# Pre-norm attention layer on one core: the weighting of the values five units behind the scores instead of three

## The chip, the core and the metric

The kernel runs on one core of one Trainium2 chip, as one program with one launch. The metric is the device time of that launch in microseconds (us). PE is the tensor engine, PEld its weight loads, ACT the scalar engine, DVE the vector engine, POOL the GpSimd engine, SP the engine that issues the DMAs (its queue is SPq in the rows).

## The reference

A pre-norm transformer layer over 4 sequences of 2048 tokens with 256 channels and 16 heads of 16 channels, all in float32. The mask is unusual: a query sees every key except the 17 from its own place back to 16 before it.

```python
def attn(x):
    qkv = einsum('bse,fe->bsf', x, in_proj_weight) + in_proj_bias
    q, k, v = split(qkv, 3)                 # 16 heads of 16
    scores = einsum('bhqd,bhkd->bhqk', q / sqrt(16), k)
    blocked = (j <= i) & (j >= i - 16)
    attn = softmax(where(blocked, -inf, scores))
    return einsum('bhqk,bhkd->bhqd', attn, v) @ out_proj_weight.T + out_proj_bias
x = x + attn(layernorm(x))
x = x + tanh(((layernorm(x) @ weight) @ aux_weight1) @ aux_weight2 + bias)
```

## The kernel before, in words

`first_batch` normalises and projects the first sequence; it ends 88 us into the span. `stream` does everything else. A guard at the end (`if_bad`) can call a slower exact path; it is not taken with these inputs.

**Units.** `stream` cuts the work into 16 steps (`NCH`), each 512 queries of one sequence. A step has 64 units (`STEP`): two passes of 8 heads (`hg`), each over 32 blocks of 64 keys (`KBLOCKS`). Unit `u` makes the scores of 512 queries against 64 keys for 8 heads. The text calls the place of a unit in its step `r` (0 to 63) and in its pass `i` (0 to 31).

- PE computes the scores of a unit in two halves, `score(u, 0)` and `score(u, 1)` (line 1183, 8 matmuls each), into two halves of one PSUM tile. It may overwrite a half once ACT has read that half of the unit before.
- ACT takes the exponential of each half (line 1160) into `probs`, a ring of 8 units (`RING`). It waits for the scores, and for the weighting of the unit that last held the ring slot.
- DVE zeroes the 17 blocked keys in the few units that hold them (`mask`, line 871; `i` of 15 to 23), two units behind.
- PE multiplies the exponentials by the values, `weigh(u)` (line 1202, 16 matmuls), and sums a pass of 32 units in the PSUM tile `outs`. The value rows have a column of ones, so `outs` also holds the sums of the softmax.
- After the last unit of a pass DVE copies `outs` to `raw` (`evacuate`, lines 879 and 880), and only then may the first `weigh` of the next pass write.

**The order is written out by hand.** Every engine walks through the same units in its own loop (`run_step`), and other work hangs at fixed values of `r`. On PE, a unit is `score(u, 0)`, then what `weighed_at(u)` names, then `score(u, 1)`, then a piece of a projection, if one is due. `weighed_at` sets how far the weighting lags: three units, with one unit without weighting after the end of a pass (`i` = 3, while DVE empties `outs`), four units behind until `i` = 12, and a double one at `i` = 13 that catches up.

**After a pass** (in step `step`, for step `f = step - 1` that has just ended): DVE empties the second pass at `r` = 3; SP moves `raw` out (`move_context`, 8 DMAs to `ctx_in` and 2 to `row_sums`), reads the sums back in another layout (line 722), and DVE inverts them at `r` = 8 (`invert`, lines 884 to 891). SP writes the inverses, reads them back spread over the channels, and DVE scales the context at `r` = 19 and 20. PE then projects it out from `r` = 23. SP issues in program order: after this chain it stores a result and loads the next inputs.

**Beside it, in steps 0 to 11**, the projection of the next sequence: PE turns the normalised input at `r` = 7 to 10 (`turn`, line 1230), DVE copies it to `s_xt` at `r` = 11 (`copy_turned`, line 924), and PE projects q and k from `r` = 12 (`project_qk`, line 1241), where its first matmul waits for that copy. DVE takes the four results at `r` = 17, 22, 37 and 42 (`take_qk`, line 935 onwards), and PE starts the next one in the same PSUM banks at `r` = 18, 33 and 38. `squash` on ACT (line 1152) is the tanh of an earlier step; DVE adds the residual at `r` = 10 (`add_squashed`, line 1048).

After unit 1023 PE has three units left to weigh; then the chain above runs once more with nothing beside it, followed by the output projection and the feed-forward part of the last step.

Of the kernel before, what the change touches and what calls it, by code (L numbers as in the profile page):

```python
# [1 line left out]

# [7 lines left out]
ALU = mybir.AluOpType  # L10
# [3 lines left out]
P = 128  # L14
# [37 lines left out]
NORM_AT = 49  # L52
F_TURN_AT = {True: (56, 57, 58, 59), False: (41, 42, 43, 44)}
# [476 lines left out]
def stream(nc, keep, lay, x, w1_t, a1_t, a2, q_parts, k_parts, row_sums, row_inverse, out):  # L530


    with ExitStack() as ctx:  # L533
# [51 lines left out]

        scored = sem("scored")
# [7 lines left out]
        floored = sem("floored")  # L594
# [8 lines left out]
        eps_added = sem("s_eps_added")  # L603
# [11 lines left out]
        v_added = sem("s_v_added")  # L615
        norms_ready = sem("s_norms_ready")
        norms_copied = sem("s_norms_copied")
        norms_added = sem("s_norms_added")
        max_done = sem("s_max_done")
        product_done = sem("s_product_done")  # L620
        worst_done = sem("s_worst_done")
        bound_done = sem("s_bound_done")
# [11 lines left out]
        y_added = sem("s_y_added")  # L634
# [3 lines left out]
        f_eps_added = sem("s_f_eps_added")  # L638
# [5 lines left out]
        f_added = sem("s_f_added")  # L644
        qk_added = sem("s_qk_added")
# [157 lines left out]
        def _(pool):  # L803
            bias = keep["bias_o"][:].unsqueeze(1).to_broadcast([P, TPC, EMB])

            def rsqrt(step):
                pool.wait_ge(stats_done, step + 1)
                pool.tensor_tensor(var_eps[:], mean_var[:, :, 1], keep["eps"][:], ALU.add).then_inc(eps_added, 1)
                pool.wait_ge(eps_added, step + 1)
# [12 lines left out]
            def f_rsqrt(c):  # L822
                pool.wait_ge(f_stats_done, c + 1)
                pool.tensor_tensor(f_var_eps[:], f_mean_var[:, :, 1], keep["eps"][:], ALU.add).then_inc(f_eps_added, 1)  # L824
                pool.wait_ge(f_eps_added, c + 1)
                pool.tensor_tensor(f_rstd[:], f_var_eps[:], keep["minus_half"][:], ALU.pow).then_inc(f_rstd_done, 1)  # L826

            def guard_of(b):

                pool.wait_ge(max_done, 2 * b + 2)  # L830
                pool.tensor_tensor(product[:], qk_max[:, 0:1], qk_max[:, 1:2], ALU.mult).then_inc(product_done, 1)
                pool.wait_ge(product_done, b + 1)
                pool.tensor_copy(keep["worst"][:, 0:2, b + 1], qk_max[:]).then_inc(worst_done, 1)
                pool.tensor_copy(keep["worst"][:, 2:3, b + 1], product[:]).then_inc(worst_done, 1)
                pool.tensor_tensor(bound[:], product[:], keep["half_power"][:], ALU.pow).then_inc(bound_done, 1)
                pool.wait_ge(bound_done, b + 1)
# [27 lines left out]
        def _(dve):  # L864
# [17 lines left out]
            def invert(c):  # L882
                dve.wait_ge(sums_in, c * 16 + 16)
                dve.tensor_scalar(sums_floor[:], sums[:], SUM_FLOOR, None, ALU.max).then_inc(floored, 1)
# [3 lines left out]
                dve.wait_ge(floored, c + 1)  # L888
# [39 lines left out]
            def take_qk(step, j):  # L928
                n = step * 4 + j
                dve.wait_ge(qk_ready, n + 1)  # L930
                if n >= 2:
# [4 lines left out]
                                  ).then_inc(qk_added, 1)  # L936
                dve.wait_ge(qk_added, n + 1)
# [12 lines left out]
            def take_v(step, half):  # L950
                b, qc = divmod(step + CPB, CPB)
                dve.wait_ge(v_ready, step * 2 + half + 1)
                if step >= CPB:
# [7 lines left out]
                        [P, 4, HALVES * HG, HD]), ALU.add).then_inc(v_added, 1)  # L961
                dve.wait_ge(v_added, step * 2 + half + 1)
# [3 lines left out]
            def take_norms(step):  # L966
# [5 lines left out]
                dve.tensor_copy(both, spare[0][0:HALF_P]).then_inc(norms_added, 1)  # L972
                dve.wait_ge(norms_added, 2 * step + 1)
                dve.tensor_tensor(both, both, spare[1][0:HALF_P], ALU.add).then_inc(norms_added, 1)
                dve.wait_ge(norms_added, 2 * step + 2)
# [17 lines left out]
            def add_attention(c, pair):  # L993
# [4 lines left out]
                                  ).then_inc(y_added, 1)  # L998
                dve.wait_ge(y_added, c * 2 + pair + 1)
# [35 lines left out]
            def add_f_bias(c, pair):  # L1035
                dve.wait_ge(f_ready, c * 2 + pair + 1)
                if c:
# [3 lines left out]
                                  keep["bias_f"][:].unsqueeze(1).to_broadcast([P, 2, EMB]), ALU.add).then_inc(f_added, 1)  # L1041
                dve.wait_ge(f_added, c * 2 + pair + 1)
# [7 lines left out]
            def run_step(step):  # L1050
# [3 lines left out]
                for r in range(STEP):  # L1054
# [45 lines left out]
                    if finishes:  # L1100
                        if r == 8:
# [67 lines left out]
        def _(pe):  # L1169
# [212 lines left out]
            for u in range(NCH * STEP, NCH * STEP + 3):  # L1382
# [677 lines left out]
```

## Time and profile before

| what | value |
|---|---|
| median of 3 runs | 2064.96 us (2062.73 to 2069.01) |
| the profiled execution's own time | 2062.95 us |
| its span, first to last instruction | 2058.0 us |
| first exponential starts / last one starts | 88.97 / 1992.8 us |
| ACT busy | 1924.7 us (94%) |
| PE busy | 1827.9 us (89%) |
| DVE busy | 696.1 us (34%) |
| POOL busy | 151.5 us (7%) |
| mean granted clock of TensorE | 0.981 of full speed |

Times in rows are from the span's start. Two instructions of ACT overlap at their ends, so that "mean ns of one" is more than busy time by count; the distance from start to start is what one costs. A number in brackets behind a row is the idle time of the engine before it, with what ended it. "x16" counts instructions merged into the row.

### The profile page before, as it was taken

Reading aid. Unit: us, or ns where it says so; the run is one execution under the profiler, and the core shown is the slowest. Engines: PE = TensorE matmul, PEld = TensorE weight load, DVE = VectorE, ACT = ScalarE, POOL = GpSimd, SP = SyncE. Lnnn points to the kernel's source line nnn. Section 1 sums busy time; section 2 is a strip of 40 time slices with the busy share of each in tenths; the row PEclk is TensorE's granted clock in tenths of the full one; section 3 lists DMA queues with packets and bytes.
Section 4 is the critical chain, followed back from the end, with each engine's and each line's share of the span. In section 5 each row is a group of like instructions: output and inputs, shape, how many; then the busy total and the mean of one; then the engine's idle time right before and its main releaser. Section 6 shows DMA issues by size and latency. Waiting matters only on the chain. (4 is left out here: it accounts for less than half of the span.)

```text
span 2058.0 us, 100762 instructions
## 1 busy us (share of the span) xinstructions
PE 1827.9 (89%) x47072; PEld 751.1 (36%) x47072; DVE 696.1 (34%) x1366; ACT 1924.7 (94%) x2106; POOL 151.5 (7%) x172
## 2 busy tenths in 40 slices
PE   6599899999999999999999999999998888898872
PEld 3233334343434334343443434343332323232321
DVE  5323332433344343434433343343322112121222
ACT  3499999999999999999999999999999999999970
POOL 1000000101010000101100010000000000000000
PEclk9799999999999999999999999999999999999995
DMA  3400102101230210202231110201111010101010
GB/s 118 137 27 23 58 26 59 36 18 55 58 100 27 58 37 18 64 25 61 57 82 45 30 61 17 60 27 54 54 54 48 13 42 12 47 16 47 8 29 24
DMA packets 93664, 94.39 MB, mean 46 GB/s; under 512 B 17514, under 2 KB 84522, under 8 KB 93234
## 3 DMA queue, kind: packets, MB, share of 16 engines
q1 hardware_dynamic: 93236, 87.84, 14.8%
q8 instruction: 372, 6.09, 1.3%
q14 instruction: 56, 0.46, 0.1%
HBM read 53.09 MB, written 26.25 MB: 39 GB/s over the span
## 5 line engine op out<-in xcount | busy, mean ns | idle before, releaser
L1160 ACT ACTIVATE probs<-scores 128x1024 f32<-128x1024 f32 x2048 | 1886.9, 1113 | 28.6 <-PE scores L1183 26.6
L1202 PE MATMUL outs<-probs,vs 64*32 64x512 f32 x16384 | 1076.5, 590 | 0.2 <-issue 0.2
L1183 PE MATMUL scores<-qs,ks 49*32 49x512 f16 x16384 | 838.6, 383 | 164.1 <-ACT probs L1160 142.9
L1183 PEld LDWEIGHTS scores<-qs,ks 49*32 49x32 f16 x16384 | 233.2, 89 | 1085.4 <-ACT probs L1160 1046.1
L1202 PEld LDWEIGHTS outs<-probs,vs 64*32 64x32 f32 x16384 | 301.2, 106 | 36.7 <-issue 11.3
L871 DVE TENSOR_TENSOR probs<-probs,allowed 128x320 f32<-128x320 f32 (+2 forms) x280 | 149.4, 537 | 308.2 <-ACT probs L1160 307.9
L1241 PE MATMUL spare<-s_xt,w_qkv 64*32 64x256 f32 x3072 | 121.4, 376 | 0.0
L1241 PE MATMUL spare<-w_o,ctx_in 64*32 64x256 f32 x2048 | 80.4, 384 | 21.0 <-DVE ctx_in L896 19.4
L820 POOL TENSOR_TENSOR s_squares<-s_qk_f 128x512 bf16<-128x512 f32 x48 | 61.3, 1278 | 353.0 <-DVE s_qk_f L938 353.0
L814 POOL TENSOR_TENSOR s_x<-s_x,bias_o 128x1024 f32<-128x1024 f32 x16 | 38.1, 2384 | 626.2 <-DMA s_x<-in_x 626.2
L1241 PE MATMUL spare<-w_ffn,s_f_xt 64*32 64x256 f32 x2048 | 81.6, 389 | 3.0 <-DVE s_pre L1043 1.6
L935 DVE TENSOR_SCALAR s_qk_f<-spare,bias_qk 128x512 f32<-128x512 f32 x48 | 36.1, 751 | 136.5 <-PE spare L1241 136.5
L997 DVE TENSOR_TENSOR s_x<-s_x,spare 128x512 f32<-128x512 f32 x32 | 22.0, 688 | 176.8 <-PE spare L1241 176.8
L1241 PEld LDWEIGHTS spare<-s_xt,w_qkv 64*32 64x32 f32 x3072 | 56.6, 106 | 26.9 <-issue 3.6
L1031 DVE COPY s_f_xt<-spare 128x512 f32<-128x512 f32 x32 | 20.6, 686 | 134.6 <-PE spare L1230 134.6
L1040 DVE TENSOR_TENSOR s_pre<-spare,bias_f 128x512 f32<-128x512 f32 x32 | 22.1, 691 | 130.0 <-PE spare L1241 130.0
L1152 ACT ACTIVATE s_pre<-s_pre 128x1024 f32<-128x1024 f32 x16 | 18.3, 1146 | 47.2 <-DVE s_pre L1043 47.2
L879 DVE COPY raw<-outs 128x512 f32<-128x512 f32 x32 | 22.1, 691 | 118.4 <-PE outs L1202 118.4
L1285 PE MATMUL spare<-w_qkv,s_xt 64*32 64x128 f32 x3072 | 61.4, 269 | 0.0
L1285 PEld LDWEIGHTS spare<-w_qkv,s_xt 64*32 64x32 f32 x3072 | 49.9, 106 | 15.5 <-issue 3.7
L1241 PEld LDWEIGHTS spare<-w_o,ctx_in 64*32 64x32 f32 x2048 | 37.4, 108 | 39.9 <-DVE ctx_in L896 20.3
L958 DVE TENSOR_TENSOR vs<-spare,bias_v 128x512 f32<-128x512 f32 x24 | 16.6, 692 | 102.5 <-PE spare L1285 102.5
(103 smaller groups left out, 770.5 us busy)
## 6 DMA issues: line engine op xcount, KB each, us to landing
qs<-q_parts SPq DMA_DIRECT2D x192, 64.0 KB
ks<-k_parts SPq DMA_DIRECT2D x192, 64.0 KB
ctx_in<-raw SPq DMA_DIRECT2D x256, 32.0 KB, 2.0
inverse<-row_inverse SPq DMA_DIRECT2D x32, 256.0 KB
s_x<-in_x SPq DMA_DIRECT2D x16, 512.0 KB, 7.2
out<-s_pre SPq DMA_DIRECT2D x16, 512.0 KB, 6.1
s_xin<-in_x SPq DMA_DIRECT2D x12, 512.0 KB, 7.8
q_parts<-s_parts SPq DMA_DIRECT2D x24, 256.0 KB, 2.3
```

Source lines behind the costliest of these rows:

```text
L814: pool.tensor_tensor(x2[:], x2[:], bias, ALU.add).then_inc(biased, 1)
L820: pool.tensor_tensor(squares[:, j], qk_f[:, j % 2], qk_f[:, j % 2], ALU.mult).then_inc(squared, 1)
L871: dve.tensor_tensor(tiles, tiles, keep_row, ALU.mult).then_inc(masked, 1)
L879: dve.tensor_copy(raw[:, 0], outs[:, 0])
L935: dve.tensor_scalar(qk_f[:, j % 2], spare[0][:], scale, bias_qk[:, j:j + 1], ALU.mult, ALU.add).then_inc(qk_added, 1)
L997: dve.tensor_tensor(tiles, tiles, spare[0][:].rearrange("p (t e) -> p t e", t=2), ALU.add).then_inc(y_added, 1)
L1040: dve.tensor_tensor(tiles, spare[0][:].rearrange("p (t e) -> p t e", t=2), keep["bias_f"][:].unsqueeze(1).to_broadcast([P, 2, EMB]), ALU.a ...
L1160: act.activation(probs[:, u % RING, 2 * slot:2 * slot + 2].rearrange("p c q -> p (c q)"), scores[:, 2 * slot:2 * slot + 2].rearrange("p c ...
L1183: last = pe.matmul(scores[cols, 2 * slot + e], ks[rows, group, keys], qs[rows, group], start=True, stop=True)
L1202: last = pe.matmul(outs[32 * c:32 * c + 32, side], vs[keys, at:at + 2 * HD], probs[keys, u % RING, c], start=(i == 0), stop=(i == KBLOCKS ...
L1241: last = pe.matmul(spare[part][32 * c:32 * c + 32, at:at + EMB], weights(rows, c), moving[rows], start=(k == 0), stop=(k == HALVES - 1))
L1285: last = pe.matmul(spare[part][32 * c:32 * c + 32, i * P:(i + 1) * P], xt[rows, k, keys], w_qkv[rows, k, 2 * EMB + side * P:2 * EMB + (sid ...
```

## The change

A new constant `LAG = 5` takes the place of the 3 in `weighed_at`, in the number of units left after the last scores, and in DVE's two places of `evacuate` (`r` 3 and 35 become 5 and 37) and of `invert` (`r` 8 becomes 10). The unit without weighting moves from `i` = 3 to `i` = 5, and the stretch that runs one unit further behind is now six behind, `i` = 6 to 12. The double one stays at `i` = 13. The diff also replaces a dozen semaphores, each of which an engine used to wait for its own last instruction, by one counter for DVE and one for POOL; each such wait still waits for the same instruction.

```diff
+LAG = 5
...
+        dve_step = sem("dve_step")
+        dve_steps = count(1)
+        pool_step = sem("pool_step")
+        pool_steps = count(1)
...
             i = position % KBLOCKS
             base = position - i
-            if i < 3:
-                found = [base - 3 + i]
-            elif i == 3:
+            if i < LAG:
+                found = [base - LAG + i]
+            elif i == LAG:
                 found = []
             elif i < 13:
-                found = [position - 4]
+                found = [position - LAG - 1]
             elif i == 13:
-                found = [position - 4, position - 3]
+                found = [position - LAG - 1, position - LAG]
             else:
-                found = [position - 3]
+                found = [position - LAG]
...
             def invert(c):
                 dve.wait_ge(sums_in, c * 16 + 16)
-                dve.tensor_scalar(sums_floor[:], sums[:], SUM_FLOOR, None, ALU.max).then_inc(floored, 1)
+                dve.tensor_scalar(sums_floor[:], sums[:], SUM_FLOOR, None, ALU.max).then_inc(dve_step, 1)
...
-                dve.wait_ge(floored, c + 1)
+                dve.wait_ge(dve_step, next(dve_steps))
...
-                    if finishes and r == 3:
+                    if finishes and r == LAG:
                         evacuate(f, 1)
-                    if r == 35:
+                    if r == KBLOCKS + LAG:
                         evacuate(step, 0)
...
-                        if r == 8:
+                        if r == LAG + 5:
                             invert(f)
...
-            for u in range(NCH * STEP, NCH * STEP + 3):
+            for u in range(NCH * STEP, NCH * STEP + LAG):
                 for w in weighed_at(u):
                     weigh(w)
```

How the instructions move. Lines of the changed kernel are 4 lower than those of the one before in this part of the file.

DVE at the start of step 2, from the end of the feed-forward bias to the copy of the turned input. Before:

```order
163 L908 BN_AGGR s_mean_var<-s_stats 128x2 x4
164 L879 COPY raw<-outs 128x512
165 L880 COPY raw<-outs 128x512
166 L915 TENSOR_SCALAR s_xin<-s_xin,s_mean_var,s_rstd 128x256 x4
167 L1040 TENSOR_TENSOR s_pre<-spare,bias_f 128x512
168 L1043 TENSOR_TENSOR s_pre<-s_pre,spare 128x512
169 L884 TENSOR_SCALAR sums_floor<-sums 128x64
170 L886 SCALAR_TENSOR_TENSOR sums_fine<-sums,sums_fine 128x64
171 L891 RECIPROCAL sums_inv<-sums_floor 128x64
172 L1048 TENSOR_TENSOR s_pre<-s_pre,s_x 128x1024
173 L924 COPY s_xt<-spare 128x8x64 x2
```

And with the change:

```order
164 L904 BN_AGGR s_mean_var<-s_stats 128x2 x4
165 L911 TENSOR_SCALAR s_xin<-s_xin,s_mean_var,s_rstd 128x256 x2
166 L875 COPY raw<-outs 128x512
167 L876 COPY raw<-outs 128x512
168 L911 TENSOR_SCALAR s_xin<-s_xin,s_mean_var,s_rstd 128x256 x2
169 L1036 TENSOR_TENSOR s_pre<-spare,bias_f 128x512
170 L1039 TENSOR_TENSOR s_pre<-s_pre,spare 128x512
171 L1044 TENSOR_TENSOR s_pre<-s_pre,s_x 128x1024
172 L880 TENSOR_SCALAR sums_floor<-sums 128x64
173 L882 SCALAR_TENSOR_TENSOR sums_fine<-sums,sums_fine 128x64
174 L887 RECIPROCAL sums_inv<-sums_floor 128x64
175 L920 COPY s_xt<-spare 128x8x64 x2
```

The copy of `outs` now stands between the two halves of the normalisation, and the inversion of the sums has passed the residual add: it is now the last thing ahead of the copy of the turned input.

PE at the end of `stream`, from the last units of scores to the output projection. Before:

```order
3363 L1183 MATMUL scores<-qs,ks 32x512 x16
3364 L1202 MATMUL outs<-probs,vs 32x512 x8
3365 L1183 MATMUL scores<-qs,ks 32x512 x8
3366 L1202 MATMUL outs<-probs,vs 32x512 x24
3367 L1241 MATMUL spare<-w_o,ctx_in 32x256 x64
```

And with the change:

```order
3359 L1179 MATMUL scores<-qs,ks 32x512 x16
3360 L1198 MATMUL outs<-probs,vs 32x512 x8
3361 L1179 MATMUL scores<-qs,ks 32x512 x8
3362 L1198 MATMUL outs<-probs,vs 32x512 x40
3363 L1237 MATMUL spare<-w_o,ctx_in 32x256 x64
```

A matmul of float32 stands in these lists once and in the trace twice, so one weighting is x8 here and x16 there. Five weightings instead of three now follow the last scores.

## Rows read from the trace of the kernel before

**Rows 1.** The page, busy time by engine.

```profile
PE 1827.9 (89%) x47072; PEld 751.1 (36%) x47072; DVE 696.1 (34%) x1366; ACT 1924.7 (94%) x2106; POOL 151.5 (7%) x172
```

**Rows 2.** Who waited for whom: total us, times, longest.

```profile
ACT probs L1160 <- PE scores L1183: 26.6, 8, 21.5
...
PEld outs L1202 <- ACT probs L1160: 0.4, 1, 0.4
```

**Rows 3.** Timeline of ACT: start, length, what, count [idle before].

```profile
88.97 8.36 ACT L1160 ACTIVATE probs<-scores 128x1024 f32<-128x1024 f32 x9 [21.47 <-PE scores L1183]
98.38 1.94 ACT L1160 ACTIVATE probs<-scores 128x1024 f32<-128x1024 f32 x2 [1.05 <-PE scores L1183]
100.65 34.23 ACT L1160 ACTIVATE probs<-scores 128x1024 f32<-128x1024 f32 x37 [0.33 <-PE scores L1183]
136.00 9.43 ACT L1160 ACTIVATE probs<-scores 128x1024 f32<-128x1024 f32 x10 [1.13 <-PE scores L1183]
...
583.10 1.15 ACT L1152 ACTIVATE s_pre<-s_pre 128x1024 f32<-128x1024 f32 x1
584.05 117.96 ACT L1160 ACTIVATE probs<-scores 128x1024 f32<-128x1024 f32 x128
```

**Rows 4.** Timeline of PE at the start of the stream.

```profile
95.94 1.93 PE L1202 MATMUL outs<-probs,vs 64*32 64x512 f32 x16
...
98.50 1.84 PE L1202 MATMUL outs<-probs,vs 64*32 64x512 f32 x16
```

**Rows 5.** Stretches there: busy of PE, PEld, DVE, ACT, POOL; granted clock; DMA share, GB/s.

```profile
94.00:96.00 2.00, 1.42 (x32) 0.38 (x32) 0.72 (x6) 2.00 (x3) 1.08 (x2) 0.50 0.02 7
...
100.00:102.00 2.00, 1.92 (x48) 0.43 (x32) 0.00 (x0) 1.67 (x3) 0.00 (x0) 0.97 0.00 0
```

**Rows 6.** Timeline at the end of the stream, PE, PEld and DVE.

```profile
1992.52 2.77 PE L1202 MATMUL outs<-probs,vs 64*32 64x512 f32 x48
1992.95 0.14 PEld L1202 LDWEIGHTS outs<-probs,vs 64*32 64x32 f32 x8 [0.29 <-issue]
1993.38 0.14 PEld L1202 LDWEIGHTS outs<-probs,vs 64*32 64x32 f32 x8 [0.29 <-issue]
...
1995.41 0.69 DVE L879 COPY raw<-outs 128x512 f32<-128x512 f32 x1 [9.41 <-PE outs L1202]
...
2013.29 1.29 DVE L896 TENSOR_TENSOR ctx_in<-ctx_in,inverse 128x512 f32<-128x512 f32 x2 [6.80 <-DMA inverse<-row_inverse]
```

**Rows 7.** Timeline of step 6, r = 2 to 12: DVE, SP and PE.

```profile
808.46 0.69 DVE L879 COPY raw<-outs 128x512 f32<-128x512 f32 x1 [1.23 <-PE outs L1202]
...
820.73 0.20 DVE L884 TENSOR_SCALAR sums_floor<-sums 128x64 f32<-128x64 f32 x1 [4.70 <-DMA sums<-row_sums]
...
820.98 0.55 DVE L891 RECIPROCAL sums_inv<-sums_floor 128x64 f32<-128x64 f32 x1
...
824.54 1.29 DVE L924 COPY s_xt<-spare 128x512 f32<-128x512 f32 x2 [1.58 <-PE spare L1230]
...
817.54 0.53 PE L1230 MATMUL spare<-ident,s_xin 64*32 64x64 f32 x32
...
827.42 0.40 PE L1183 MATMUL scores<-qs,ks 49*32 49x512 f16 x8
827.64 0.62 PE L1241 MATMUL spare<-s_xt,w_qkv 64*32 64x256 f32 x16
```

**Rows 8.** The same two places in step 9, the one with the earliest sums.

```profile
1175.21 0.20 DVE L884 TENSOR_SCALAR sums_floor<-sums 128x64 f32<-128x64 f32 x1 [2.80 <-DMA sums<-row_sums]
...
1184.01 0.62 PE L1241 MATMUL spare<-s_xt,w_qkv 64*32 64x256 f32 x16
```

**Rows 9.** Timeline of step 6, r = 36 to 39, PE and DVE.

```profile
870.77 1.04 PE L1202 MATMUL outs<-probs,vs 64*32 64x512 f32 x16
...
872.60 0.75 DVE L935 TENSOR_SCALAR s_qk_f<-spare,bias_qk 128x512 f32<-128x512 f32 x1 [3.03 <-PE spare L1241]
...
875.51 0.62 PE L1241 MATMUL spare<-s_xt,w_qkv 64*32 64x256 f32 x16
```

More of the change, by code:

```diff
@@ L1 @@
 from contextlib import ExitStack
+from itertools import count
 import concourse.bass as bass
@@ L593, in stream @@
         sums_in = sem("sums_in")
-        floored = sem("floored")
         inverted = sem("inverted")
@@ L633, in stream @@
         y_ready = sem("s_y_ready")
-        y_added = sem("s_y_added")
         x2_done = sem("s_x2_done")
@@ L807, in rsqrt @@
                 pool.wait_ge(stats_done, step + 1)
-                pool.tensor_tensor(var_eps[:], mean_var[:, :, 1], keep["eps"][:], ALU.add).then_inc(eps_added, 1)
-                pool.wait_ge(eps_added, step + 1)
+                pool.tensor_tensor(var_eps[:], mean_var[:, :, 1], keep["eps"][:], ALU.add).then_inc(pool_step, 1)
+                pool.wait_ge(pool_step, next(pool_steps))
                 pool.tensor_tensor(rstd[:], var_eps[:], keep["minus_half"][:], ALU.pow).then_inc(rstd_done, 1)
@@ L823, in f_rsqrt @@
                 pool.wait_ge(f_stats_done, c + 1)
-                pool.tensor_tensor(f_var_eps[:], f_mean_var[:, :, 1], keep["eps"][:], ALU.add).then_inc(f_eps_added, 1)
-                pool.wait_ge(f_eps_added, c + 1)
+                pool.tensor_tensor(f_var_eps[:], f_mean_var[:, :, 1], keep["eps"][:], ALU.add).then_inc(pool_step, 1)
+                pool.wait_ge(pool_step, next(pool_steps))
                 pool.tensor_tensor(f_rstd[:], f_var_eps[:], keep["minus_half"][:], ALU.pow).then_inc(f_rstd_done, 1)
@@ L960, in take_v @@
                     keep["bias_v"][:].rearrange("p (n d) -> p n d", d=HD).unsqueeze(1).to_broadcast(
-                        [P, 4, HALVES * HG, HD]), ALU.add).then_inc(v_added, 1)
-                dve.wait_ge(v_added, step * 2 + half + 1)
+                        [P, 4, HALVES * HG, HD]), ALU.add).then_inc(dve_step, 1)
+                dve.wait_ge(dve_step, next(dve_steps))
                 dve.tensor_tensor(columns, columns, spare[1][:].rearrange("p (k n d) -> p k n d", k=4, d=HD),
@@ L971, in take_norms @@
                     dve.wait_ge(max_done, 2 * b)
[L972 to L975, printed above, removed]
+                dve.tensor_copy(both, spare[0][0:HALF_P]).then_inc(dve_step, 1)
+                dve.wait_ge(dve_step, next(dve_steps))
+                dve.tensor_tensor(both, both, spare[1][0:HALF_P], ALU.add).then_inc(dve_step, 1)
+                dve.wait_ge(dve_step, next(dve_steps))
                 for w in range(2):
@@ L1040, in add_f_bias @@
                 dve.tensor_tensor(tiles, spare[0][:].rearrange("p (t e) -> p t e", t=2),
-                                  keep["bias_f"][:].unsqueeze(1).to_broadcast([P, 2, EMB]), ALU.add).then_inc(f_added, 1)
-                dve.wait_ge(f_added, c * 2 + pair + 1)
+                                  keep["bias_f"][:].unsqueeze(1).to_broadcast([P, 2, EMB]), ALU.add).then_inc(dve_step, 1)
+                dve.wait_ge(dve_step, next(dve_steps))
                 dve.tensor_tensor(tiles, tiles, spare[1][:].rearrange("p (t e) -> p t e", t=2), ALU.add
```

24 lines of the change are left out of this document (8 added, 16 removed).

## The prediction, written before the changed kernel was run

> **What bounds the kernel now.** The page's busy times come first [rows 1]: ACT is busy 94% of the span and PE 89%, so either could set the pace. The list of who waited for whom decides between them [rows 2]. ACT waited for scores 8 times, 26.6 us in all, and 21.5 us of it is one wait, the start of the stream, which the first row of ACT's timeline shows [rows 3]. That leaves 5.1 us of idle ACT in 1904 us of stream. PE's weighting never waited for DVE's masks: no such row exists, and its one wait for ACT is 0.4 us [rows 2]. Next the timeline of ACT [rows 3]: 128 exponentials in a row take 117.96 us, (117.96 - 1.13) / 127 = 0.92 us from start to start, the 1.13 being the length of the last one. A unit is two of them, 1.84 us. The stream is 2048 times 0.92 us plus 15 tanh of 0.95 us (583.10 to 584.05), and the change touches none of these. ACT is the bound; PE and DVE matter only where they make it wait, and after its last exponential.
>
> **The change part by part.**
>
> *The lag itself, in the stream: 0 us.* Weighting five units back instead of three gives ACT's results and DVE's masks 3.68 us more to be ready. Nobody waits for them, so there is nothing to gain. The ring of 8 still holds: ACT needs the slot of unit u - 8, and at six behind that one is weighed in unit u - 2, ahead of `score(u - 2, 1)` on PE. Three exponentials, 2.8 us, lie between it and the one that needs the slot. The unit that is left empty and the double one are the same work as before, one of them two units later. PE's sum over the stream is unchanged.
>
> *The end: +1.7 us.* After the last scores PE has three weightings left, 48 matmuls in 2.77 us [rows 6], and nothing runs beside them but the last exponential. DVE's copy of `outs` starts 0.12 us behind them, and everything to the end hangs on it in one chain. Now five are left. Their price is read between two groups of weight loads: 8 of them from 1992.95 to 1993.38, so 0.43 us for eight matmuls and 0.86 us for one weighting (3 x 0.86 + 0.19 for the last matmul to drain is 2.77). Two more are +1.72 us, all of it on the path. Bounds: 2 x 0.86 and 2 x 1.04, the latter being a weighting with its drain [rows 9], so 1.7 to 2.1.
>
> *The start: +0.8 us.* Two places in the first units cost ACT 1.05 and 0.33 us [rows 3]. They stand where PE weighs for the first time at a granted clock of 0.5, which is 1.2 GHz: a weighting takes 1.93 and then 1.84 us there, and 1.04 us at 2.4 GHz [rows 4, 5, 9]. Before 95.94 PE had only scores (1.42 us busy in 2) and the clock stayed at 0.5; it rose about 4.2 us after the first weighting, at about 100.1. With the change the first weighting stands at `r` = 6, 3.68 us later, at about 99.6. If the clock again rises some 4 us behind it, the same two stalls come 3.68 us later. They then meet the first turn of the input at `r` = 7, which takes 0.53 us at full clock [rows 7] and about twice that at half. I take the same 1.4 us plus 0.8 us, between those two. Bounds: below, the clock is already up and both stalls go, -1.4; above, one more unit with a turn runs at half clock: 1.3 us of scores (1.42 busy in 2 us [rows 5]) + 1.84 + 1.06 = 4.2 us against 1.84, so about +2.4.
> The Trainium skill (TensorE: Matmul & The Clock Gate, Part 1) says that the moment of the rise differs from run to run, since the gate's own timing is not tied to the kernel's start, and advises not to fit to one cold count. By that rule the term has no fixed value and may fall anywhere between the bounds just given; the one profiled execution here cannot show the spread.
>
> *DVE's two moves: 0 us, with a cover that becomes thin.* The second pass is emptied 3.68 us later, and so is the whole chain on SP behind it. Step 6 is the tightest of steps 2 to 11 [rows 7]. There the sums arrive at 820.73 and the inversion ends at 821.53. With the change they arrive at about 824.41, and DVE, which works in order, stands at the inversion until then. Behind it is the copy of the turned input: 824.41 + 0.80 + 1.29 = 826.50. PE wants that copy at 827.64, and may ask from 827.42 on. The margin falls from 1.6 us (the copy ended at 825.83) to 0.9 us. In step 9, the best, the sums are 8.80 us ahead of the projection instead of 6.91 [rows 8], so the margin is 2.8 us. All ten steps lie between these. The residual add, which the inversion used to precede, now stands ahead of it; it waits only for the tanh of `r` = 8, so it is over before the sums come.
> Further down the chain, the context is scaled at `r` = 19, seven units behind 827.64, at about 840.5. The tail shows how long the chain takes with nothing in its way: from the copy at 1995.41 to the scaling at 2013.29, 17.9 us [rows 6]. From the copy at 808.46 + 3.68 that is 830.0, 10 us early. The input load and POOL's bias add behind them have until `r` = 27. For the first pass, the copy of `outs` moves to `r` = 37, directly ahead of the third q/k result [rows 9]. The last weighting of the pass ends at 871.8, so the copies run to about 873.2, and the result that is taken from 872.60 on is taken 0.6 us later. PE needs it at 875.51; two instructions of some 0.75 us behind 873.2 end at 874.7, so 0.8 us of cover is left.
>
> *The merged semaphores: 0 us.* The same number of waits on the same instructions; bound 0 from both sides, since each counter only moves on its own engine in program order.
>
> **The sum.** Profiled execution 2062.95 + 1.7 + 0.8 = 2065.5 us. The median of the runs shown lies 2.0 us above the profiled one, so I give 2067.5 us, +0.12%. A difference of 0.3%, 6.2 us, is about what a measurement of this kernel can tell from none; the three runs span 6.3 us.
>
> **The rivals.**
>
> *Slower: the projection waits behind the inversion of the sums.* If the sums come more than 0.9 us later than step 6 has them, PE stands at its first q/k matmul in `r` = 12, the next scores are late, and ACT stops. For it: the cover is the thinnest of the change, and the wait is a DMA's, whose time from the sums' issue to DVE's start differs from step to step. Against it: the margin in the row is positive in the worst step and 2.8 us in the best, and the transfers keep their order. Price: sums 2 us later than in step 6, in each of 11 steps, is 11 x (2.0 - 0.9) = 12 us, 2079 us. It passes 0.3% from 0.35 us per step on, on top of the 2.5 us of the sum.
> The Trainium skill (DMA: Bandwidth & Descriptors, Latency and other measured facts) gives the access time of HBM as 0.2 us on average and 2 us at high load. Taken for each arrival in place of the rows, a swing of 1.8 us beyond step 6 would give this rival; the rows show less.
>
> *The clock is up in time.* The scores alone lift the clock before `r` = 6, and both stalls at the start go: 2067.5 - 0.8 - 1.4 = 2065.3 us. For it: PE has been at work 11 us by then. Against it: from 94 to 96 us it was as busy with scores as it will be two units later, and stayed at 0.5 [rows 5].
>
> *Faster: the slack helps after all.* Every wait of ACT for scores in the stream goes, 5.1 us: 2064.96 + 1.7 - 5.1 = 2061.6 us, which is still within 0.3%. For it: PE has more freedom in what it may do next. Against it: two of these waits, 1.13 us each, stand behind full-width matmuls that fold the weights in step 0 (the exponential at 136.00 [rows 3]), which the change leaves where they are. To be faster by over 0.3% the stream would have to lose 7.9 us, more than its idle time.
>
> **How the numbers follow.** Forecast 0.79, slower rival 0.08, clock 0.09, slack 0.04. The range, 2063 to 2073, takes in the bounds of both terms (2064.96 + 1.7 - 1.4 = 2065.3 to 2064.96 + 2.1 + 2.4 = 2069.5) and 2 to 4 us of run scatter to either side. Slower by over 0.3% is the rival with a little for scatter, 0.09; faster 0.03 is scatter and the slack case; within 0.3% is 0.88.
>
> **What would show it.** Right: 80 matmuls of weighting in about 4.5 us after the last scores, and the copy of `outs` about 4.6 us after them; first exponentials x13 in one run before a stall instead of x9; 118.7 us from tanh to tanh in steps 3 to 10; the copy to `s_xt` no longer waiting for PE's turn but directly behind the reciprocal. Wrong: a row in which PE's projection waits for `s_xt`, or ACT waits for scores at `r` = 12 or 13 in several steps, or a start that loses more than 4 us; on the other side, ACT's idle time in the stream under 3 us.

## The result and the profile after

| what | before | changed |
|---|---|---|
| median of 20 runs each | 2063.51 us | 2068.78 us |
| lowest to highest | 2058.88 to 2071.70 | 2064.21 to 2074.75 |
| ratio to before | | 1.0023, 95% interval 1.0012 to 1.0034 |
| profiled execution | 2062.95 us | 2065.40 us |
| its span | 2058.0 us | 2061.1 us |

The changed kernel is slower by 0.23%, clear of zero and under the 0.3% that was called no change. The forecast was 0.12% slower, and the time lies in its range. In microseconds the medians stand 5.3 us apart, where the forecast had 2.5. A second comparison (below) gave 1.0030 (1.0012 to 1.0047).

The page of the changed kernel, busy time by engine, beside [rows 1]:

```profile
PE 1827.5 (89%) x47072; PEld 751.9 (36%) x47072; DVE 708.2 (34%) x1366; ACT 1925.7 (93%) x2106; POOL 151.9 (7%) x172
```

The work is the same. The list of who waited for whom, beside [rows 2] (total us, times, longest):

```profile
DVE raw L875 <- PE outs L1198: 209.4, 32, 18.1
...
DVE s_pre L1044 <- ACT s_pre L1148: 87.0, 16, 5.9
DVE sums_floor L880 <- DMA sums<-row_sums: 53.6, 13, 10.2
...
ACT probs L1156 <- PE scores L1179: 28.8, 10, 22.3
```

DVE now waits at other places, as its new order has it, and that costs nothing. What counts is the last row: ACT waited for scores ten times instead of eight, 6.5 us behind the first wait instead of 5.1. The timeline of ACT says where, beside [rows 3]:

```profile
88.02 12.02 ACT L1156 ACTIVATE probs<-scores 128x1024 f32<-128x1024 f32 x13 [22.25 <-PE scores L1179]
101.02 32.40 ACT L1156 ACTIVATE probs<-scores 128x1024 f32<-128x1024 f32 x35 [0.98 <-PE scores L1179]
134.54 9.43 ACT L1156 ACTIVATE probs<-scores 128x1024 f32<-128x1024 f32 x10 [1.13 <-PE scores L1179]
...
701.10 1.15 ACT L1148 ACTIVATE s_pre<-s_pre 128x1024 f32<-128x1024 f32 x1
702.05 14.16 ACT L1156 ACTIVATE probs<-scores 128x1024 f32<-128x1024 f32 x15
717.41 103.90 ACT L1156 ACTIVATE probs<-scores 128x1024 f32<-128x1024 f32 x113 [1.20 <-PE scores L1179]
821.08 1.15 ACT L1148 ACTIVATE s_pre<-s_pre 128x1024 f32<-128x1024 f32 x1
```

The first row holds 13 exponentials, as forecast, and one stall of 0.98 us behind them. The row at 717.41 is new. The tanh of a step ends `r` = 8, so 15 exponentials from 702.05 lead to the second half of `r` = 16: ACT stood there for 1.20 us in step 5. PE around it:

```profile
714.65 1.03 PE L1198 MATMUL outs<-probs,vs 64*32 64x512 f32 x11
716.10 0.62 PE L1198 MATMUL outs<-probs,vs 64*32 64x512 f32 x3 [0.41 <-issue]
```

In the middle of one weighting PE stops after 11 of 16 matmuls, and starts again at 716.10. It waits for no engine and for no DMA that the program knows ("issue"). Matmuls overlap, so the idle time in brackets is short; from the last start before the stop, at 715.1, to the next is 1.0 us.

The end of the stream, beside [rows 6]:

```profile
1994.17 4.48 PE L1198 MATMUL outs<-probs,vs 64*32 64x512 f32 x80
1994.61 0.14 PEld L1198 LDWEIGHTS outs<-probs,vs 64*32 64x32 f32 x8 [0.29 <-issue]
1995.03 0.14 PEld L1198 LDWEIGHTS outs<-probs,vs 64*32 64x32 f32 x8 [0.29 <-issue]
...
1998.78 0.69 DVE L875 COPY raw<-outs 128x512 f32<-128x512 f32 x1 [11.12 <-PE outs L1198]
```

80 matmuls in 4.48 us instead of 48 in 2.77: 1.71 us more. The place where the cover was called thin, here in step 5, beside [rows 7]:

```profile
702.28 1.23 DVE L1044 TENSOR_TENSOR s_pre<-s_pre,s_x 128x1024 f32<-128x1024 f32 x1 [5.86 <-ACT s_pre L1148]
703.42 0.19 DVE L880 TENSOR_SCALAR sums_floor<-sums 128x64 f32<-128x64 f32 x1
...
705.09 1.29 DVE L920 COPY s_xt<-spare 128x512 f32<-128x512 f32 x2 [0.88 <-PE spare L1226]
...
707.10 0.45 SPq L745 DMA_DIRECT2D out<-s_pre  x1
707.60 0.51 SPq L741 DMA_DIRECT2D s_x<-in_x  x1
708.15 1.07 SPq L761 DMA_DIRECT2D s_xin<-in_x  x1
708.19 0.62 PE L1237 MATMUL spare<-s_xt,w_qkv 64*32 64x256 f32 x16
```

The copy of the turned input ends at 706.4, 1.8 us ahead of PE, and still waits a little for PE's turn. The prediction had named the contrary as a sign of being right, the copy directly behind the reciprocal; that is so in four of steps 2 to 11, and in the other six the copy still waits for PE. The least margin was 1.0 us, in step 9:

```profile
1183.23 1.22 DVE L920 COPY s_xt<-spare 128x512 f32<-128x512 f32 x2
...
1185.46 0.62 PE L1237 MATMUL spare<-s_xt,w_qkv 64*32 64x256 f32 x16
```

No row of this profile has PE waiting for `s_xt`. The three rows of SP in step 5 matter below: 1.5 MB of bulk transfers, a result out and two inputs in, issued just when the projections begin.

### The profile page after: what moved, and what is told of

It reads as the page before. It is cut to its first block and busy times, and to the rows that moved or that the text cites. A ratio compares the mean times of both kernels' runs of the same rounds, so it can differ in the third digit from the quotient of the medians.

```text
span 2061.1 us, 100762 instructions
## 1 busy us (share of the span) xinstructions
PE 1827.5 (89%) x47072; PEld 751.9 (36%) x47072; DVE 708.2 (34%) x1366; ACT 1925.7 (93%) x2106; POOL 151.9 (7%) x172
## 5 line engine op out<-in xcount | busy, mean ns | idle before, releaser
L1156 ACT ACTIVATE probs<-scores 128x1024 f32<-128x1024 f32 x2048 | 1887.8, 1111 | 31.1 <-PE scores L1179 28.8
L867 DVE TENSOR_TENSOR probs<-probs,allowed 128x320 f32<-128x320 f32 (+2 forms) x280 | 157.8, 568 | 281.3 <-ACT probs L1156 280.8
L943 DVE SCALAR_TENSOR_TENSOR s_parts<-s_qk_f,s_parts 128x512 f16<-128x512 f32 x48 | 52.3, 1090 | 0.8
```

What stands on the lines that cost most here:

```text
L867: dve.tensor_tensor(tiles, tiles, keep_row, ALU.mult).then_inc(masked, 1)
L943: dve.scalar_tensor_tensor(out=parts[:, j, 1], in0=qk_f[:, j % 2], scalar=SCALE_UP, in1=parts[:, j, 0], op0=ALU.mult, op1=ALU.subtract).th ...
L1156: act.activation(probs[:, u % RING, 2 * slot:2 * slot + 2].rearrange("p c q -> p (c q)"), scores[:, 2 * slot:2 * slot + 2].rearrange("p c ...
```

## The experiments

Each ran beside the kernel before on the same chip, and the ratio is to that: the medians of before were 2064.36, 2063.77 and 2063.32 us in the three later groups of runs. "Stream" is the distance from the first exponential's start to the last one's, by the timeline of ACT; "end" is from there to the end of the span. Each is of one profiled execution; "stalls" are ACT's waits for scores between `r` = 13 and 19 of steps 1 to 11.

| kernel | median us | ratio (95%) | stream | end | stalls |
|---|---|---|---|---|---|
| before | 2063.51 | 1 | 1903.8 | 65.2 | 0.3 |
| before, again | 2062.05 | 0.9993 (0.9976 to 1.0009) | 1905.4 | 64.3 | 2.1 |
| changed | 2068.78 | 1.0023 (1.0012 to 1.0034) | 1906.4 | 66.7 | 1.8 |
| changed, again | 2071.38 | 1.0030 (1.0012 to 1.0047) | 1908.7 | 66.4 | 4.1 |
| lag 5, end 3 | 2068.74 | 1.0020 (1.0006 to 1.0035) | 1908.9 | 64.9 | 2.6 |
| lag 3, bulk late | 2064.81 | 1.0006 (0.9994 to 1.0019) | 1905.2 | 65.3 | 0.8 |
| lag 3, 192 more PE instructions ahead | 2069.72 | 1.0021 (1.0000 to 1.0041) | 1908.4 | 63.4 | 4.2 |
| lag 3, spread | 2060.84 | 0.9987 (0.9975 to 0.9999) | 1902.9 | 65.2 | 0.4 |
| lag 3, spread, again | 2060.60 | 0.9996 (0.9982 to 1.0010) | 1902.9 | 63.8 | 0.2 |
| lag 5, spread | 2065.04 | 1.0009 (0.9994 to 1.0023) | 1902.0 | 65.8 | 0.0 |
| lag 5, spread, end 3 | 2062.35 | 0.9995 (0.9980 to 1.0010) | 1904.1 | 63.7 | 0.0 |
| lag 3, spread, fold in pieces | 2061.33 | 0.9994 (0.9980 to 1.0007) | 1900.7 | 65.4 | 0.0 |
| lag 5, sums late | 2105.26 | 1.020 (one run) | 1944.4 | 67.6 | 37.4 |

**Both kernels again.** No edit.

> The kernel before, unchanged, against itself, to see what a comparison of this kind scatters by. Every theory expects a ratio of 1.000 with an interval that holds it. In the profile: three weightings (48 matmuls) in 2.77 us after the last scores, ACT idle for scores in the stream (the waits after the first) some 5 us, of which 2 x 1.13 us stand at the folds of step 0. If the rest of these waits stands at other places than in the first profile, then they are chance events of PE and not places of the program.

> The changed kernel, unchanged. All theories expect 1.0012 to 1.0034 as in the first comparison. Theory A (the end): the loss that comes back in every profile is the 1.72 us of the two weightings after the last scores. Theory B (a collision): the bulk loads and stores that SP now issues two units later meet a dense part of PE's program, and PE is short of instructions at r = 15 to 17 of several steps (in the first profile three steps of ten, 1.8 us in all); then stalls at r = 15 to 17 are there again, in 2 to 5 steps. Theory C (chance): such stalls are as many and as long as in the kernel before, at other places, and the difference of the two streams has another size or sign this time.

The loss came back. With two profiles of each, the span grew by 4.4 us: the stream by 2.9, the end by 1.8, less 0.3 for an earlier first exponential. The medians differ by more, 7.0 us here: the profiled executions of the changed kernel were the second fastest of its 20 and of its 12 runs, those of before near the middle of theirs, so the profiles understate the loss. Theory A, the end alone, is out. The stalls of the changed kernel came back at the same places: `r` = 17 of step 4, 16 of step 5, 58 of step 7 and 43 of step 13, in both profiles. Places that repeat belong to the program; the size varies. The kernel before has its own: `r` = 58 of step 11 in both, and 13 to 15 in some steps:

```profile
949.63 0.60 PE L1241 MATMUL spare<-s_xt,w_qkv 64*32 64x256 f32 x9
951.02 0.42 PE L1241 MATMUL spare<-s_xt,w_qkv 64*32 64x256 f32 x4 [0.79 <-issue]
```

This timeline of PE is of the kernel before, again, in step 7, `r` = 14: the same stop with "issue" inside a group of equal matmuls.

What PE waits for there shows when the stops are laid beside the queue "instruction" of the page (queue 8, packets of 16 KB). These landings are taken from the DMA records of the traces:

```
kernel            packet landed   PE starts again   between
before                1504.93         1506.38         1.45
before, again          949.69          951.02         1.33
changed                314.92          316.42         1.50
changed                714.65          716.10         1.45
changed               1030.23         1031.65         1.42
changed, again         715.81          717.27         1.46
changed, again        1313.96         1315.35         1.39
```

Each time PE starts again 1.3 to 1.5 us behind the landing of a packet. The list can be made complete: in the twelve profiles without late sums, PE stood 0.5 us or more from one start to the next 30 times with no engine behind it (a repeated row at the start of steps 13 to 15, which costs ACT nothing, left out), and 29 of the 30 stops ended 1.2 to 1.6 us behind a landing. The reading is that PE had run out of instructions. A count speaks for these packets being PE's own: 372 packets in the span, at 256 instructions each, make 95,232, and PE ran 94,144 matmuls and weight loads. A packet lasts about 5 us here. The Trainium skill (Runtime: NRT & Kernel Launch, Instruction fetch mechanics) describes these blocks of 16 KB with 256 instructions, and holds that the sequential fetch is hidden, since instructions are issued slower than they are filled in. The block size agrees with the records; the second part does not hold for this kernel, whose unrolled PE program stood for up to 1.3 us at such a block in the profiles listed above.

This reading, that PE's instructions come late, is theory D of the expectations below.

**The end alone.** The weighting catches up in the last pass; the rest is the changed kernel.

```diff
+        def lag_into(p):
+            return 3 if p == NCH * HALVES else LAG
...
+                upto = max(done - 1, at - lag_into(p + 1))
+            most = 2 if i in (13, 17 if p % 2 == 0 else 16, 22 if p % 2 == 0 else 18) else 1
```

> The changed kernel, but in the last pass of 32 units PE catches up with two more double weightings, so that only three are left after the last scores, as before. Theory A expects all of the steady loss gone at this place: 48 matmuls in 2.8 us instead of 80 in 4.5 us, the time 1.7 us under the changed kernel's, ratio to before about 1.0015 if the rest is real and 1.000 if it is chance. Theory B expects 1.7 us less too, but the stream's stalls at r = 15 to 17 unchanged, ratio 1.001 to 1.002.

48 matmuls in 2.77 us again, and the end 64.9 us instead of 66.5. The median is 2.6 us under the changed kernel's on the same chip. The stream keeps its loss; 0.8 us of it are stalls of the two new double weightings at `r` = 49 and 51. So the end's term is confirmed by the timeline, and something else is at least as large.

**Only the bulk transfers late.** The kernel before, with one wait on SP:

```diff
                     invert_sums(step - 1)
+                    sp.wait_ge(scored, begun + 26)
                     if step > 1:
                         store_result(step - 2)
                     start_chunk(step - 1)
```

> The kernel before with one wait added on SP, so that the store of a result and the two loads of inputs in each step are issued when the scores of r = 12 are done, 3.7 us later than before and where the changed kernel issues them; the lag stays three and the end is as before. Theory B expects its stalls here as well: ACT waits for scores at r = 15 to 17 in 2 to 5 steps, 1 to 3 us in all, ratio 1.0005 to 1.0015. Theories A and C expect 1.000 and no stall tied to those places.

Inconclusive as to time: 1.0006 with 1 inside. No stall stood at `r` = 13 to 15; there was one at `r` = 19 of step 3 and one at `r` = 17 of step 8, so the time of the transfers has a part in the place. But they summed to 0.8 us, under the 1 to 3 us that theory B had asked for: in this one profile, late transfers under the old PE program are not enough for the changed kernel's loss.

**Where the blocks begin.** The kernel before with 192 more PE instructions ahead of the stream:

```diff
+            for n in range(96):
+                pe.matmul(spare[0][0:32, 0:32], head_of[:, 0], head_of[:, 0], start=True, stop=True)
             for step in range(NCH):
                 run_step(step)
```

> The kernel before with 96 small matmuls (192 PE instructions of 64 bytes) ahead of the first scores; they write a PSUM bank that nobody reads yet. From r = 6 on the changed kernel's PE program stands 64 instructions earlier for a given unit than before, which modulo the 256 instructions of a 16 KB packet is the same as 192 later. Theory D expects the stalls at the changed kernel's places, in a kernel with a lag of three: near r = 58 in steps 1 and 7 and near r = 43 in step 13, and no longer near r = 58 in steps 5 and 11; those of r = 13 to 19 move too. If packets have no part in it, the places stay those of before (step 5 and 11, r = 58). The time is 3 to 6 us longer for the 96 matmuls themselves, less up to 1 us if they lift the clock earlier.

Timeline of ACT of this kernel, steps 7 and 8:

```profile
942.48 90.68 ACT L1160 ACTIVATE probs<-scores 128x1024 f32<-128x1024 f32 x98
1033.52 27.77 ACT L1160 ACTIVATE probs<-scores 128x1024 f32<-128x1024 f32 x30 [0.37 <-PE scores L1183]
```

98 exponentials behind the tanh is `r` = 58 of step 7, the changed kernel's place, in a kernel with a lag of three. `r` = 43 of step 13 appeared too (0.28 us), and the stall at `r` = 58 of step 11, which both profiles of before have, is gone. One of the places expected, `r` = 58 of step 1, did not come. Near `r` = 13 to 19 it has its own set, 4.2 us in all, and 3.3 us of it is one event in step 8:

```profile
1080.40 0.40 PE L1183 MATMUL scores<-qs,ks 49*32 49x512 f16 x4 [1.85 <-issue]
...
1082.00:1084.00 2.00, 2.00 (x40) 1.26 (x32) 0.71 (x2) 1.51 (x2) 0.00 (x0) 0.50 0.13 44
```

The first line is of the timeline of PE, the second a stretch with the columns of [rows 5]. PE started again 1.6 us behind the landing of a packet, and then the granted clock fell to 0.5 from 1081.4 to 1084.8, so that ACT stood four times, 1.83 us and then 1.42 us more at the low clock. The stream of this kernel is 1908.4 us, 3.8 us more than the mean of before, with a lag of three and the transfers at their old time; the extra matmuls lie ahead of it. The ratio, 1.0021 (1.0000 to 1.0041), includes them. So where the blocks of 256 begin decides the places, and can by itself cost as much as the lag did. The lag shifts the blocks by 64 instructions: two weightings of 32 stand behind a given unit instead of ahead of it.

**The bulk transfers spread.** One edit on SP, in the kernel before and in the changed one. The load of the residual input waits for the scores of `r` = 17 (not in steps 4, 8 and 12), and the load of the next projection's input moves behind the stores of q and k, to about `r` = 24:

```diff
                     if step > 1:
                         store_result(step - 2)
+                    if qc:
+                        sp.wait_ge(scored, begun + 36)
                     start_chunk(step - 1)
-                if step + 1 < PROJECTED:
-                    sp.wait_ge(turned, step + 1)
-                    sp.dma_start(xin[:], x_tiles[CPB + step + 1]).then_inc(x_in, 16)
...
                     store_part(step, 0)
                     store_part(step, 1)
+                if step + 1 < PROJECTED:
+                    sp.wait_ge(turned, step + 1)
+                    sp.dma_start(xin[:], x_tiles[CPB + step + 1]).then_inc(x_in, 16)
```

> The kernel before, but SP spreads the bulk transfers of a step: the load of the residual input waits for the scores of r = 17 (except in steps 4, 8 and 12, where it stays), and the load of the next projection's input stands behind the second q/k store, r = 23. Theory D (instruction fetch, formed on the profiles so far): PE stands because its next 16 KB of instructions come late, a packet that shares the DMA engines with these bulk transfers; then ACT's stalls between r = 13 and 19 (2.1 us in the second profile of before, 0.3 in the first) go to under 0.4 us, those near r = 58 stay (1.2 us), ratio 0.999 to 1.000. A theory by which these stalls come from DVE or from the projections' own waits expects them unchanged.

> The changed kernel with the same spreading of the bulk transfers. Theory D expects the stalls at r = 15 to 17 (1.8, 4.1 and 2.6 us in the three profiles with a lag of five) to fall under 0.5 us, those near r = 58 and r = 43 to stay (1.5 us), and the time to fall by 2 to 3 us to a ratio of 1.0010 to 1.0015 over before: what is left is the end, 1.7 us, and scatter. Were the stalls a matter of the lag itself, they stay and the ratio stays at 1.002 to 1.003.

> The spread kernel with a lag of three again, on this chip beside the others: 0.998 to 1.000 of before, stalls of ACT between r = 13 and 19 under 0.5 us, those at r = 58 in steps 5 and 11 again there.

As to the stalls, this is the run that decides. With a lag of five those of `r` = 13 to 19 are gone and the stream is 1902.0 us, 5.5 us less than the mean of the two changed profiles. One part of the expectation missed: the stalls near `r` = 58 and 43 were to stay at 1.5 us, and only one of 0.3 us was left. The loss over before is 0.09%, 1 inside its interval, after 0.23 and 0.30%. Timeline of ACT in the same step 5:

```profile
700.56 1.15 ACT L1150 ACTIVATE s_pre<-s_pre 128x1024 f32<-128x1024 f32 x1
701.51 117.95 ACT L1158 ACTIVATE probs<-scores 128x1024 f32<-128x1024 f32 x128
819.24 1.16 ACT L1150 ACTIVATE s_pre<-s_pre 128x1024 f32<-128x1024 f32 x1
```

128 exponentials in 117.95 us, the free pace of [rows 3]. The DMA engines in that stretch of step 5, first of the changed kernel, then of the spread one; the columns are those of [rows 5], and the last but one is the share of the 16 DMA engines that is busy:

```profile
708.00:710.00 2.00, 2.00 (x64) 0.86 (x54) 0.00 (x0) 2.00 (x3) 0.00 (x0) 1.00 0.92 250
710.00:712.00 2.00, 2.00 (x56) 0.72 (x48) 0.00 (x0) 2.00 (x3) 0.00 (x0) 1.00 0.98 289
712.00:714.00 2.00, 2.00 (x72) 1.01 (x64) 0.00 (x0) 1.95 (x3) 0.00 (x0) 1.00 1.03 349
714.00:716.00 2.00, 1.69 (x43) 0.39 (x30) 0.68 (x1) 2.00 (x3) 1.48 (x1) 1.00 0.32 106
```

```profile
707.50:709.50 2.00, 2.00 (x68) 0.87 (x59) 0.00 (x0) 2.00 (x3) 0.00 (x0) 1.00 0.85 257
709.50:711.50 2.00, 2.00 (x56) 0.72 (x48) 0.00 (x0) 2.00 (x3) 0.00 (x0) 1.00 0.54 176
711.50:713.50 2.00, 2.00 (x72) 1.01 (x64) 0.00 (x0) 1.95 (x3) 0.00 (x0) 1.00 0.08 26
```

Full for 6 us in the one, the better part of 2 us in the other. The packet whose landing at 714.65 PE needed began at 713.50, 7.9 us behind the one before it; in the spread kernel the packets of this stretch began 4.7 and 4.8 us apart. Between `r` = 10 and 19 of steps 1 to 11, a distance of over 7.5 us came once in each profile of before, three, five and four times in the three with a lag of five and the transfers as they were, twice with the transfers late alone, and never in the five spread ones. Over steps 2 to 11, worked out from the DMA records, the engines are fullest at `r` = 12 and 13 before (0.97, 0.96), at `r` = 14 and 15 in the changed kernel (1.00, 0.95), and nowhere over 0.75 between `r` = 10 and 19 in the spread ones. From `r` = 14 on, PE has a piece of the projections of q and k in nearly every unit.

With a lag of three the spread gave 0.9987 and 0.9996; the first interval ends at 0.9999, the second holds 1. Its stream was 1902.9 us both times, against 1903.8 and 1905.4, but a gain over the kernel before is not established.

Like against like, the time is less clear than the stalls. Both spread kernels ran on the same chip, and their medians differ by 4.2 us (2065.04 and 2060.84), against 5.3 and 7.0 us for the lag without the spread; resampling the eleven runs of each puts the ratio between 1.0004 and 1.0041. The end accounts for 1.7 us of it. The profiled execution with a lag of five was the fastest of its eleven, so its rows cannot show what the slower ones lost. The trace shows that the spread removes these stalls; how much of the median it takes away is not settled.

**Both repairs in the changed kernel.** The spread edit and the three units left at the end.

> The changed kernel with both repairs: the bulk transfers spread as in the two kernels before, and three units instead of five left after the last scores. If instruction fetch (theory D) and the end (theory A) are the whole loss, nothing of the lag's cost is left: the time is that of the spread kernel with a lag of three, within what the runs scatter by, ratio to before 0.998 to 1.000. If something else in the lag costs time, it stays 1 us or more above that kernel.

0.9995 (0.9980 to 1.0010), as fast as the kernel before. It is 1.75 us above the spread kernel with a lag of three on the same chip. By the letter of the expectation, 1 us or more speaks for something else in the lag, but twelve runs of each cannot tell a difference of that size from none. Of its stream, 0.8 us are again the stalls at `r` = 49 and 51 of the last step, which the catching up brings in. Whether anything of the lag's cost is left stays open; it is under what these runs can tell.

**The thin cover, broken.** The changed kernel, with the sums read late in steps 1 to 11:

```diff
                 sp.wait_ge(sums_out, (step + 1) * 64)
+                if step < PROJECTED - 1:
+                    sp.wait_ge(scored, 2 * STEP * (step + 1) + 24)
```

> The changed kernel, but in steps 1 to 11 SP reads the sums only when the scores of r = 11 are done, some 5 us later than it could, which breaks the cover that the prediction called thin. By the prediction's reckoning the sums come near 828.4 in step 6's terms instead of 823.4, the copy of the turned input ends near 830.5, 3 us after PE asks for it, and ACT loses 2.5 to 3 us in each of 11 steps, 28 to 33 us in all, ratio 1.015 to 1.018. If the order behind the inversion does not matter, nothing is lost.

2105.26 us in its one run, 1.020 of the median of before and 34 to 37 us over the changed kernel's medians. Its waits:

```profile
ACT probs L1158 <- PE scores L1181: 63.6, 36, 21.8
...
PE spare L1239 <- DVE s_xt L922: 23.0, 11, 2.8
```

PE waited 11 times for `s_xt`, 2.1 us each, and ACT lost (63.6 - 28.8) / 11 = 3.2 us per step at `r` = 13 and 14. The slower rival of the prediction is a real mechanism; in the change its condition was not met. PE waited less than the 3 us expected, and yet ACT lost more than the 2.5 to 3 us. The steps differ, and stretches of step 1 and step 7, again with the columns of [rows 5], show why:

```profile
236.00:238.00 2.00, 2.00 (x32) 0.83 (x24) 0.00 (x0) 1.02 (x1) 0.00 (x0) 0.50 0.27 95
```

```profile
972.00:974.00 2.00, 2.00 (x56) 0.84 (x48) 0.00 (x0) 1.91 (x2) 0.00 (x0) 1.00 0.38 106
```

In nine of the eleven steps the granted clock fell to 0.5 just behind PE's wait, and ACT lost 3.3 to 3.6 us, 5.7 us in step 9. In steps 7 and 10 the clock stayed up, and ACT lost 1.6 and 1.8 us, a little less than PE had waited (1.9 and 2.1). So the wait itself costs ACT no more than its length; the rest is the low clock behind it, which neither the prediction nor the expectation had priced.

**A version with less.** The spread kernel with a lag of three, and the folding of the weights in step 0 in eight pieces:

```diff
-FOLD_AT = (23, 28)
+FOLD_AT = ((23, 24, 25, 26), (28, 29, 30, 31))
...
-                for half in range(HALVES):
-                    for k in range(HALVES):
+                half, k = divmod(i, HALVES)
```

> The spread kernel with a lag of three, and the folding of the feed-forward weights in step 0 cut into eight pieces of 0.5 us at r = 23 to 26 and 28 to 31 instead of two of 2 us. The two waits of ACT of 1.13 us in step 0 go; 2.2 us less than the spread kernel, 2058 to 2059 us, ratio to before about 0.9975. If a piece of full-width matmuls costs more beside the other work than a projection's piece of 0.53 us, some 0.1 us per piece stays.

Both stalls of 1.13 us are gone and the stream is 2.2 us shorter than in the spread kernels. Step 0 gave only 1.5 us of that, since ACT still slips there by 1.2 us in waits too short to be listed; the rest is in the other steps. The profiled execution was 2057.9 us, the lowest of the profiled ones, but its median of 12 runs, 2061.33, does not stand below the spread kernel's 2060.60. A gain of 2 us is under what these comparisons can tell.

## Why the prediction was right, and where it was not

The range and the bound held the result, and the profiled execution came out at 2065.4 us against a sum of 2065.5. That agreement is partly luck: of the sum's terms, one held, one was not there, and a third was missing. The second profiled execution was 2067.7 us, and both medians, 2068.8 and 2071.4 us, stand above the 2067.5 that was given.

- **The bound** held. ACT sets the pace at 0.92 us an exponential, undisturbed steps take 118.7 us, and neither PE nor DVE became the bound.
- **The end, +1.7 us**, held: 1.71 us in the timeline, 1.8 us in the means of two profiles, and it went when the last pass caught up.
- **The start, +0.8 us**, was wrong. The stalls there were 0.98 and 1.05 us in the two changed profiles against 1.38 and 1.05 before. The step that failed is "if the clock again rises some 4 us behind it". The first weighting began at 98.66; the windows of the changed kernel:

```profile
98.00:100.00 2.00, 1.74 (x24) 0.57 (x32) 0.00 (x0) 2.00 (x3) 0.00 (x0) 0.50 0.03 8
100.00:102.00 2.00, 2.00 (x40) 0.41 (x24) 0.00 (x0) 1.02 (x3) 0.00 (x0) 0.82 0.00 0
```

A mean of 0.82 over 100 to 102 is 0.5 until about 100.7 and 1.0 after, so the clock rose 2 us behind the first weighting, not 4.2. One slow weighting was left instead of two; in the second profile of the kernel before there was also only one. Over all thirteen profiles the distance was 2.1 to 4.2 us, and the one that the prediction had read was the longest; the second stall came only in the two where it was over 4 us. By the rule of the Trainium skill (TensorE: Matmul & The Clock Gate, Part 1) that the moment is not tied to the program, the term should have been left at its bounds, and the spread of the thirteen agrees; a single observed distance was no estimate.
- **DVE's two moves, 0 us**, held. The copy was ready at least 1.0 us ahead, where 0.9 was reckoned for the worst step. But the worst step was 9, which the prediction called the best with 2.8 us: the copy waits for PE's turn as well, so that 1.8 us is the most there can be, and step 6 had it. Moving each arrival by the same 3.68 us did not give the order of the steps.
- **The merged semaphores, 0 us**, were not tested by themselves: every kernel with a lag of five has them, none with a lag of three.
- **The lag itself, in the stream, 0 us**, was wrong, and it is the larger miss: 2.9 us. The reckoning covered waits between engines and the work on each. It took "PE's sum over the stream is unchanged" for enough. What moved was the program against its own 16 KB blocks, and SP's bulk transfers against the dense part of PE's program. The prediction said that the whole chain on SP comes two units later and priced it only by who needs the data, not by what else uses the DMA engines then. The hint stood in the profile of before: a stop of PE with "issue" in it that ended at 1506.38 and cost ACT 0.97 us.
- **The slower rival** did not happen, and was shown to cost 34 to 37 us where its condition is forced. Its price counted PE's wait alone and had no term for the clock, which fell behind PE's wait in nine steps of eleven.

What stays open: how much of the 2.9 us is the place of the transfers and how much the place of the blocks. Late transfers alone cost nothing clear (1.0006), shifted blocks alone moved the stalls and lengthened the stream by 3.8 us in one profile, and both together are the changed kernel. That the spread removes the stalls of `r` = 13 to 19 shows that the transfers are needed for those, not that they suffice; the ones near `r` = 58 come without them. The size varies by as much as 2.3 us between two profiles of one kernel. And the medians of the two spread kernels still stand 4.2 us apart, of which the profiles explain the 1.7 us of the end.

## What to carry to other kernels

A software pipeline is worth deepening only where the profile shows the consumer waiting; here nobody waited, so a deeper lag could only cost, first of all two more units to drain at the end. When a change delays a chain of DMAs, look at what the DMA engines carry at the new time, the instruction stream included. A stop with "issue" in the middle of equal matmuls is a line to follow: lay it beside the landings of the instruction queue before calling it noise. When an engine's wait is priced, look at the granted clock behind it too: here the same wait of PE cost ACT twice as much where the clock fell. And one profile is one run: see where it stands among the runs of its kernel before a difference of a few microseconds is read off it.

## What the runs showed of the hardware

- PE's instructions come in packets of 16 KB over the same 16 DMA engines as the data, about one in 5 us here. When a packet began 7.9 us behind the one before it, with the engines 92 to 100% busy, PE stood still. Of 30 such stops of 0.5 us or more, 29 ended 1.2 to 1.6 us after a landing. The stalls of ACT from step 1 on came to 1.5 to 5.5 us of 2060 in a profile, and to 0.3 to 1.5 us with the transfers spread.
- The places of such stops repeat from run to run and move with the number of instructions ahead of them: 192 more moved one from step 11 to step 7, at the same `r` = 58.
- The granted clock rose from 1.2 to 2.4 GHz between 2.1 and 4.2 us behind the first weighting, in thirteen profiles; 7.7 to 11.3 us of scores alone ahead of it had not raised it in twelve of them. In the one with extra matmuls ahead it was up at 91.5 us and fell again at 95.0, under scores alone.
- Behind a wait of PE of some 2 us in full work the clock fell to 1.2 GHz in nine of eleven steps, and with that ACT lost 3.3 to 5.7 us instead of 1.6 to 1.8.
